# Attention scores of a fused mLSTM and MLP kernel from split, stacked q and k that pass through device memory

## What is computed

```python
xn = _layernorm(x)
x = x + attn(xn) + ghost_ffn(xn)     # ghost_ffn: three matmuls whose weights come from a table of 16 values
# attn: RMS norm, then with 8 heads of dqk = 32, dv = 64
q, k, v, o_pre, i_pre, f_pre = h_in @ (wq, wk, wv, w_og, w_ig, w_fg)
Dmat = Fcum[..., :, None] - Fcum[..., None, :] + i_pre[..., None, :]     # causal
qk = jnp.einsum('bhsd,bhtd->bhst', q, k) / jnp.sqrt(jnp.float32(dqk))
C = qk * jnp.exp(Dmat - m)
n = jnp.maximum(jnp.abs(jnp.sum(C, axis=-1, keepdims=True)), jnp.exp(-m))
h = jnp.einsum('bhst,bhtd->bhsd', C / n, v)
# then a norm per head, the output gate, @ w_out, RMS norm, and an MLP of width 2048
```

## Time and profile before

| | us |
|---|---|
| median of three runs | 2475.16 (2471.98 to 2475.67) |
| the profiled execution | 2471.92 |
| its span, first to last instruction | 2470.1 |
| TensorE busy | 2416.0 (98%) |
| VectorE busy | 1253.8 (51%) |
| ScalarE busy | 914.9 (37%) |
| GpSimd busy | 610.8 (25%) |

### The profile page before, as it was taken

One profiled execution on the slowest core, in us unless ns is written; L12 is line 12 of the kernel. 1 busy time (PEld: TensorE's weight loads), 2 busy tenths in 40 slices (PEclk: granted clock), 3 DMA queues, 4 the chain that ended last, 5 costly groups with the idle time before them and its releaser, 6 DMA issues. The chain is left out here.

```text
span 2470.1 us, 33080 instructions
## 1 busy us (share of the span) xinstructions
PE 2416.0 (98%) x11376; PEld 1947.6 (79%) x11376; DVE 1253.8 (51%) x2205; ACT 914.9 (37%) x1683; POOL 610.8 (25%) x499
## 2 busy tenths in 40 slices
PE   7999999999999999999999999999999999999998
PEld 5677787787787778778777877888888888888887
DVE  6776536765773675577367557743222222222222
ACT  5433245355454535545443544554111111111111
POOL 2346523221321322232132223222111111111111
PEclk9999999999999999999999999999999999999999
DMA  5055554473464448356444825676867867867865
GB/s 210 1 199 207 216 226 140 167 275 127 152 213 182 154 166 281 107 172 208 167 162 165 293 102 174 208 265 223 279 237 273 282 241 260 296 241 255 287 221 198
DMA packets 115513, 508.34 MB, mean 206 GB/s; under 512 B 11120, under 2 KB 11120, under 8 KB 80144
## 3 DMA queue, kind: packets, MB, share of 16 engines
q1 hardware_dynamic: 110016, 496.46, 57.2%
q10 hardware_dynamic: 5328, 9.70, 1.3%
HBM read 417.39 MB, written 87.69 MB: 204 GB/s over the span
## 5 line engine op out<-in xcount | busy, mean ns | idle before, releaser
L747 PE MATMUL up_bank<-act_hi,gud 128*128 128x512 f32 x1728 | 591.8, 403 | 0.0
L747 PE MATMUL gate_bank<-act_hi,gud 128*128 128x512 f32 x1728 | 574.7, 393 | 2.7 <-DVE th L1587 2.7
L2073 POOL TENSOR_TENSOR hidden_lo<-hm,hidden_hi 128x512 fp32r<-128x512 f32 x216 | 281.9, 1305 | 1136.3 <-ACT hidden_hi L1131 1136.3
L947 PE MATMUL acc<-gud,hidden_hi 128*128 128x512 f32 x1728 | 436.2, 394 | 0.9 <-ACT hidden_hi L1131 0.9
L1587 DVE SCALAR_TENSOR_TENSOR th<-th,gate_bank 128x512 f32<-128x512 f32 x216 | 147.9, 685 | 514.3 <-ACT th L1126 514.2
L1131 ACT ACTIVATE hidden_hi<-hm 128x512 fp32r<-128x512 f32 x216 | 135.9, 629 | 692.6 <-PE acc L950 681.2
L747 PEld LDWEIGHTS up_bank<-act_hi,gud 128*128 128x128 f32 x1728 | 324.6, 188 | 81.0 <-issue 13.5
L747 PEld LDWEIGHTS gate_bank<-act_hi,gud 128*128 128x128 f32 x1728 | 324.3, 188 | 75.1 <-DVE th L1587 4.6
L947 PEld LDWEIGHTS acc<-gud,hidden_hi 128*128 128x128 f32 x1728 | 319.5, 188 | 68.1 <-issue 4.2
L747 PE MATMUL up_bank<-act_lo,gud 128*128 128x512 f32 x864 | 337.7, 391 | 0.0
L747 PE MATMUL gate_bank<-act_lo,gud 128*128 128x512 f32 x864 | 336.7, 390 | 0.0
(11 more groups left out here) (326 smaller groups left out, 2973.0 us busy)
## 6 DMA issues: line engine op xcount, KB each, us to landing
gud<-mlp_parts SPq DMA_DIRECT2D x112, 1024.0 KB, 5.1
gud<-ghost_parts SPq DMA_DIRECT2D x88, 1024.0 KB, 5.9
gud<-mlp_parts SPq DMA_DIRECT2D x112, 512.0 KB, 3.9
gud<-ghost_parts SPq DMA_DIRECT2D x88, 512.0 KB, 4.6
ghost_parts<-look_w SPq DMA_DIRECT2D x35, 512.0 KB, 3.8
mlp_parts<-gud SPq DMA_DIRECT2D x16, 1024.0 KB, 3.9
vo_w_hi<-vo_parts SPq DMA_DIRECT2D x13, 1024.0 KB, 7.1
vo_w_lo<-vo_parts SPq DMA_DIRECT2D x13, 1024.0 KB, 9.9
```

The source lines that it names most:

```text
L747: mm = pe.matmul(dst, l[a], r[c], start=first and k == 0 and n == 0, stop=last and k == len(lhs) - 1 and n == 2)
L947: pe.matmul(ACC[i][:], HH[0][:, toks(i)], W3[:, z, 2, n, :], start=t == 0 and n == 0, stop=False)
L2073: pool.tensor_tensor(HH[1][:], hm[:], HH[0][:].bitcast(f32), ALU.subtract).then_inc(of.low.sem, 1)
```

## The change

The scores of every half-block but `FIRST` (7 x 8 = 56 units) are made another way. `qkT_` now makes the high parts of q and k of block i (one copy of 128 x 512, `GB` to `stack[:, i % 2, 0]`) and a float32 copy of q alone (`qT`); VectorE makes the low parts, `GB` minus the high ones, in `stack[:, i % 2, 1]` (`qkT_lo`, new). SP stores both, 256 KB each, to `qk_parts` in device memory (`store_qk`, new), in its list behind `store_xt`. From there each unit's operands are fetched (`load_qk`, new): six DMAs of 32 partitions x 4 heads x 128, 64 KB each, which put three copies of 32 rows on top of each other, (q high, q high, q low) against (k high, k low, k high) on partitions 0 to 95. SP issues them for units 0 and 1 behind the stores; ScalarE issues those of units 2 to 7, in tiles 1 to 6 after the unit's exponentials. TensorE then makes the scores of one unit with four `float32r` matmuls of 96 rows x 128 columns, one for each head, into the four quarters of the same bank. `qbd` is no longer built for these units. `stack` holds both the parts on their way out and the fetched operands, so `qkT_(2)` waits until block 0 has been stored, `qkT_(3)` until block 1 has, and `q_k_T(i)` waits for the low parts of block i - 1.

```diff
+        qk_parts = nc.dram_tensor("qk_parts", (4, NB, P, G * P), f32, kind="Internal").ap()
-        qkT = sb("qkT", [P, 2, G, TOK])
+        qT = sb("qT", [P, G, TOK])
+        stack = sb("stack", [P, 2, 2, HG * P], f32r)
+        def load_qk(e, at, u):
+            i, g = u // G, u % G
+            if u < 2:
+                e.wait_ge(st_qk[u], stacked(at, NB // 2))
+            else:
+                wait(e, pe_unit, at, u - 2, "scores")
+            for r, parts in enumerate((slice(0, 3, 2), slice(0, 4, 3), slice(1, 3))):
+                dst = stack[r * DQ:(r + 1) * DQ, u % 2, :, :].bitcast(f32).rearrange("d z (h n) -> d z h n", h=HG)
+                src = qk_parts[parts, i, :, g * P:(g + 1) * P].rearrange("z (h d) n -> d z h n", h=HG)
+                for z in range(2):
+                    e.dma_start(dst[:, z], src[:, z]).then_inc(ld_qk[u % 2], 16)
# SP
+            def store_qk(at, i):
+                wait(sp, vec_qkT, at, i, "lo")
+                for part in range(2):
+                    src = stack[:, i % 2, part, :].bitcast(f32).rearrange("p (z n) -> p z n", z=2)
+                    sp.dma_start(qk_parts[part::2, i].rearrange("z p n -> p z n"), src).then_inc(st_qk[i % 2], 16)
                             store_xt(b * HALVES + half, XH[half])
+                            for i in range(NB):
+                                store_qk(at, i)
+                            for u in range(2):
+                                load_qk(sp, at, u)
# TensorE, q_k_T(at, i)
                 if i:
-                    wait(pe, act_qkT, at, i - 1, "k")
+                    wait(pe, act_qkT, at, i - 1, "done")
+                    if not here(at, FIRST):
+                        wait(pe, vec_qkT, at, i - 1, "lo")
# TensorE, unit_1(at, u)
-                elif u:
+                pe.wait_ge(ld_qk[u % 2], stack_loaded(at, u))
+                if u:
                     wait(pe, vec_unit, at, u - 1, "update")
-                pe.matmul(pick(at, u, B, ACC[1])[:], qkT_of(at)[:, 1, g, toks(j)], pick(at, u, qbd, qbd2)[:, :, :], start=True, stop=True)\
-                    .then_inc(pe_unit.sem, 1)
+                for h in range(HG):
+                    mm = pe.matmul(B[:, toks(h)], stack[0:3 * DQ, u % 2, 1, toks(h)], stack[0:3 * DQ, u % 2, 0, toks(h)],
+                                   start=True, stop=True)
+                mm.then_inc(pe_unit.sem, 1)
# TensorE, units_first
+                unit_2(FIRST, u)
                 if 3 <= u < 7:
                     q_k_T(SECOND, u - 3)
-                unit_2(FIRST, u)
# ScalarE
             def qkT_(at, i):
                 wait(act, pe_qkT, at, i)
...
+                if i >= 2:
+                    act.wait_ge(st_qk[i % 2], stacked(at, i // 2))
+                act.activation(stack[:, i % 2, 0, :], GB[:], ACT.Copy).then_inc(act_qkT.sem, 1)
+                act.activation(qT[:, :, i * P:(i + 1) * P], both[:, 0], ACT.Copy).then_inc(act_qkT.sem, 1)
                     if stage and t < UNITS:
                         unit(at, t)
+                        if 1 <= t < UNITS - 1:
+                            load_qk(act, at, t + 1)
...
-                    if t + 1 < UNITS:
-                        qbd_(at, t + 1)
# VectorE
+            def qkT_lo(at, i):
+                wait(dve, act_qkT, at, i, "done")
+                dve.tensor_tensor(stack[:, i % 2, 1, :], GB[:], stack[:, i % 2, 0, :].bitcast(f32), ALU.subtract)\
+                    .then_inc(vec_qkT.sem, 1)
                 else:
+                    qkT_lo(at, 0)
+                    qkT_lo(at, 1)
                     dve.wait_ge(st_mlp[1 - at[1]], at[0] * 16)
                 gate_sum(at)
+                if not here(at, FIRST):
+                    qkT_lo(at, 2)
                 gate_maxima(at)
+                if not here(at, FIRST):
+                    qkT_lo(at, 3)
# VectorE, units_first
                     weights(at, u)
+                    if u in (4, 5, 6, 7):
+                        qkT_lo(SECOND, u - 4)
```

More of the change, by code:

```diff
@@ L267, in kn_, with qT_of @@
             return kn_first if here(at, FIRST) else kn
-        def qkT_of(at):
-            return qkT_first if here(at, FIRST) else qkT
+        def qT_of(at):
+            return qkT_first[:, 0, :, :] if here(at, FIRST) else qT
         qkT_first = first_rows[:, 8:12, :].rearrange("p (z g) n -> p z g n", z=2)
@@ L317, in program @@
         st_vo = sem("st_vo")
+        st_qk = [sem(f"st_qk{i}") for i in range(2)]
+        ld_qk = [sem(f"ld_qk{i}") for i in range(2)]
         ld_idx = [sem(f"ld_idx{i}") for i in range(2)]
@@ L352, in program @@
         act_qk = Steps(sem("act_qk"), NB, ["q", "k"])
-        act_qkT = Steps(sem("act_qkT"), NB, ["q", "k"])
+        act_qkT = Steps(sem("act_qkT"), NB, ["part", "done"])
         act_v = Steps(sem("act_v"), NB, ["done"])
@@ L606, in _ @@
             store_xt(1, XH[1])
+            for i in range(NB):
+                store_qk(SECOND, i)
+            for u in range(2):
+                load_qk(sp, SECOND, u)
             wait(sp, vec_norm, FIRST, NB - 1, "gated")
@@ L832, in unit_2 @@
                     wait(pe, vec_unit, at, u - 2, "state")
-                pe.matmul(pick(at, u, B, ACC[1])[:, 0:HG * VS], qkT_of(at)[:, 0, g, toks(j)], kv[:, g, :, :], start=True, stop=True)
+                pe.matmul(pick(at, u, B, ACC[1])[:, 0:HG * VS], qT_of(at)[:, g, toks(j)], kv[:, g, :, :], start=True, stop=True)
                 for h in range(HG):
@@ L856, in ho_T @@
                 else:
-                    wait(pe, act_qkT, SECOND, NB - 1, "k")
+                    wait(pe, act_qkT, SECOND, NB - 1, "done")
+                    wait(pe, vec_qkT, SECOND, NB - 1, "lo")
                 f = hn[:, :, :].rearrange("p h d -> p (h d)")
@@ L907, in gate @@
                 if t == 0 and stage:
-                    wait(pe, act_qkT, stage, NB - 1, "k")
+                    wait(pe, act_qkT, stage, NB - 1, "done")
+                    wait(pe, vec_qkT, stage, NB - 1, "lo")
                 else:
@@ L1277, in qkT_ @@
                 wait(act, pe_qkT, at, i)
[L1278 to L1281, removed]
+                both = GB[:, :].rearrange("p (z g n) -> p z g n", z=2, g=G)
+                if here(at, FIRST):
+                    for z in range(2):
+                        act.activation(qkT_first[:, z, :, i * P:(i + 1) * P], both[:, z], ACT.Copy).then_inc(act_qkT.sem, 1)
+                    return
+                if i >= 2:
+                    act.wait_ge(st_qk[i % 2], stacked(at, i // 2))
+                act.activation(stack[:, i % 2, 0, :], GB[:], ACT.Copy).then_inc(act_qkT.sem, 1)
+                act.activation(qT[:, :, i * P:(i + 1) * P], both[:, 0], ACT.Copy).then_inc(act_qkT.sem, 1)
             def v(at, i):
@@ L1335, in qbd_ @@
                 j, g = u // G, u % G
[L1336 to L1343, removed]
+                if u >= 2:
+                    wait(act, pe_unit, at, u - 2, "scores")
+                wait(act, act_qkT, at, j, "part")
                 for h in range(HG):
-                    act.activation(pick(at, u, qbd, qbd2)[:, h, :], qkT_of(at)[:, 0, g, j * P:(j + 1) * P], ACT.Copy,
+                    act.activation(pick(at, u, qbd, qbd2)[:, h, :], qkT_first[:, 0, g, j * P:(j + 1) * P], ACT.Copy,
                                    scale=bdm[:, h:h + 1]).then_inc(act_qbd.sem, 1)
@@ L1366, in units_first @@
                     unit(FIRST, u)
+                    if u in (4, 5, 6, 7):
+                        qkT_(at, u - 4)
                     if u + 2 < UNITS:
```

17 lines of the change are left out of this document (11 added, 6 removed).

## The result

| | before | after |
|---|---|---|
| median of 4 runs (range), us | 2474.44 (2471.98 to 2475.67) | 2508.61 (2505.33 to 2512.34) |
| span of the profiled execution, us | 2470.1 | 2506.4 |
| TensorE busy, us | 2416.0 | 2408.4 |
| mean granted clock | 0.995 | 0.986 |

The change makes the kernel slower: ratio 1.014, 95% interval 1.0122 to 1.0157. The forecast of the median was 2509 us.

What follows compares the result with a forecast made beforehand. TensorE, busy 2416.0 of 2470.1 us, was taken as the bound. Profiled 2471.9 - 20 (scores) + 51 (six fronts' stalls and clock) + 3 (low parts) = 2505.9; the median, 3.2 above: 2509 us, range 2494 to 2524 (8 in 10: 2470 to 2534).

Steps and rivals of the forecast that it cites:

- The wait in the front: Loop fronts: block 0's store lands behind five 1 MB DMAs on SP's queue; TensorE stands 6.9 us before `q_k_T(3)`.
- The clock behind it: After each front's stall, eight 512-column matmuls run at the lower clock, losing 1.6 us, bounds 0 and 3.4.
- What TensorE saves: Scores of 56 units: four short matmuls take 0.50 us instead of 0.86, saving 20 us, between 0 and 35.
- rival (a): Scores: the four matmuls gain nothing, the type being slow at 128 columns, and the stall stands: 2529 us; 18 in 100.
- nothing, while its idle time in a tile lasts: ScalarE in a tile: four `qbd` copies fewer, six DMA issues at 0.34 us more, 0.8 us net, costing nothing.
- Low parts in `units_first`: VectorE in `units_first`: four low parts of 0.68 us, 2.8 us counted in full, bounds 0 and 4.
- No second stall, fetches covered: Front: TensorE reaches `factors` with 1.5 us to spare; first fetches land near 800, unit 0's scores come at 809.5.
- 3.5 us of a tile: Fetches of units 2 to 7: each has a tile to land in and uses 3.5 us of it.
- rival (e): Tiles: a unit's six fetches, served one after the other, come late, TensorE waits in 42 units: 2551 or more; 4 in 100.
- Rival (b): Fronts: block 0's DMAs are served between the big ones, landing near 774, no stall: 2458 us; 13 in 100.

Runs made afterwards that it cites:

- Experiment 1: Changed kernel with SP storing blocks 0 and 1 ahead of the 1 MB DMAs in the loop's fronts, blocks 2, 3 and first fetches before `store_xt`: 2457.87 us.
- experiment 3: Kernel before, with only one wait added: in the loop's fronts `qkT_(2)` on ScalarE waits until the last 1 MB store has landed: 2511.35 us, ratio 1.0151.
- Experiment 4: Changed kernel with both operands of the four score matmuls read as plain `f32` instead of `float32r`: 2526.59 us, ratio 1.0204 to the kernel before.
- experiment 5: Changed kernel, but in `SECOND` SP instead of ScalarE issues the fetches of units 2 to 7: 2503.02 us, ratio 1.0114 to the kernel before.
- experiment 8: Changed kernel with blocks 0 and 1 stored first and SP issuing all fetches of units 2 to 7, in `SECOND` and loop: 2448.97 us, ratio 0.9896 to before.
- Experiment 2: Changed kernel, SP's order kept, but ScalarE issues the stores of blocks 0 and 1 on its own queue in the loop's fronts: 2504.82 us, ratio 1.0124 to before.

## Why the prediction was right, step by step

- *The wait in the front.* Right in place, number and chain. Forecast 6.9 us in each of six; measured 6.25 in the mean, and 6.55 in the front it was worked out for. Experiment 1 removes it by order alone, experiment 3 makes it alone.
- *The clock behind it.* Right in kind, low in size. Forecast 1.6 us a front; measured 1.4 in the front it was worked out for and 2.0 in the mean of six. The start of `q_k_T(3)` moved by 6.5 in the mean, a little more than the recorded wait. Fronts in sum: 51 forecast, 51.4 measured, with a wait somewhat too long and a clock loss somewhat too short.
- *What TensorE saves.* 0.36 us a unit forecast from the four transposes, 0.40 measured. The matmuls run at the pace of those transposes; the 81 ns each that the Trainium skill gives (TensorE: Matmul & The Clock Gate, Back-to-back issue gap) would be 0.32 for four, and the trace has 0.46. Experiment 4 settles rival (a): without the type nothing is saved.
- *Where the saving stayed.* The saving was counted in all 56 units. In the loop it came (-17.8 for 48 units), in `SECOND` it was eaten. The step that failed, there alone, is "nothing, while its idle time in a tile lasts": a fetch's issue takes 0.45 us in the median where 0.34 was counted, six of them 2.8 to 4.4 us in `SECOND`, and there ScalarE stands ahead of GpSimd and VectorE in the splitting of weights. `SECOND` lost 1.15 us where the saving of eight units, 2.9, was forecast, 4.0 us worse, and experiment 5 gives back 5.6 (5.3 against its own before). In the loop the same issues are free, as forecast (experiment 8).
- *Low parts in `units_first`.* Counted in full, 2.8 us, and no run shows that cost. After lags by 2.2 us from the second mark of `FIRST` to its fourth and by 1.6 at the first unit of `SECOND` (155.12 to 156.72), behind all four low parts; experiment 3, which has none of them, by 2.0 and 1.8. VectorE had the room.
- *The start as a whole.* It came out some 2.8 us later than the sum had it (2.75 against 2.8 - 2.9): 1.8 by the clock's dip near 17 us, which no term had, 4.0 by `SECOND`, and 3.0 less by the low parts and the rest of `FIRST`.
- *No second stall, fetches covered.* Right in outcome: the scores waited 0.2 us for a fetch, once in the whole trace. The cover is thinner than "3.5 us of a tile": a fetch lands 2.1 us after its issue in the median (1.7 to 8.1), but the last of a unit's six lands 8.0 us after the first is issued (4.6 to 10.4), 2 us ahead of the scores in the median. Six such landings one after the other, rival (e), would take 12 us or more, so they overlap. The 2.0 us that the prediction cites there stands in the Trainium skill for DMAs that GpSimd issues, and these are issued by SP and ScalarE.
- *Rival (b), the store slips between the big ones.* The rows of landing showed one queue, and within one queue the order holds. Experiment 2 shows that on a second queue it does slip in, and at 1 KB against 8 KB that did not shorten the waits (37.6 us against 37.5).

The median came to 2508.6 against 2509, closer than the working deserves. The profiled execution took 2508.6 where the sum had 2505.9: 2.8 us more at the start, 0.4 more in the fronts, 0.5 less in the loop's units. The 3.2 us by which the median of before lay above its profiled execution did not come again, and the two errors cancel. That the last microseconds agree is luck.

## What to carry to other kernels

When a change hangs a wait on a store, read what is ahead of that store on its queue before anything else: here the order of one queue was worth 51 us, more than twice what the faster matmuls bring, and with the small stores first the change is a gain of 0.7%, and with `SECOND`'s fetches on SP as well of 1%. A second queue is no way past big transfers when its own packets are small. And where ScalarE, GpSimd and VectorE hand work on in a row, half a microsecond per DMA issue on the first of them can end as a wait of TensorE two engines further on.

## What the runs showed of the hardware

- In these traces two busy queues share the DMA engines in about equal numbers of pieces, whatever their size: 302 against 283 with 8 KB and 1 KB, 281 against 279 with 8 KB and 2 KB.
- VectorE's 128 x 512 operations with both inputs in SBUF take 0.69 us alone and 1.66 to 2.10 beside GpSimd's. The one that starts at 197.58 ends 0.54 us after GpSimd's `MX` operation (197.25 + 1.89 = 199.14), and the next, from 199.72, 0.55 after GpSimd's `gud` (199.10 + 1.73 = 200.83): they end as if each had stood until GpSimd's was through. The Trainium skill (SBUF — State Buffer, Who interferes with whom) says that a VectorE instruction with two SBUF inputs contends with a GpSimd instruction that reads SBUF, for ports held as an exclusive lock. The rows agree; the overlap cost 1.4 us of the first and 1.0 of the second.
- `float32r` still pays at 128 columns: four matmuls with their loads take 0.46 us, 0.89 in plain `f32`. But it does not keep its rate: the same 512 columns in one matmul take 0.23.
- The granted clock fell to the lower level in each stall of 5.6 to 7.0 us, and four to ten 512-column matmuls behind it still ran 0.43 us apart, not 0.23. The same stall cost 1.4 us in one front and 2.6 in another.
- A DMA issue of 32 x 4 x 128 elements holds ScalarE's queue for 0.45 us in the median (0.31 to 1.46), where those of the earlier trace rows took 0.34. The view by lines of after (ns min/median/max):

```profile
L531 ACTq DMA_DIRECT2D stack<-qk_parts x252: 309/453/1459, 166.4 to 1548.7; - x126
```
